# A fused attention, expert and scan network on one core: the blocks are divided twelve to four between the two sets of expert tiles instead of eleven to five

## What is computed

```
# 1 x = x + delta_rule_attention(norm(x))       16 heads of 16
# 2 expert layer: 32 experts, each token goes to 8 of them, plus a shared one
g = jnp.einsum('th,eih->eti', x, expert_gate)
u = jnp.einsum('th,eih->eti', x, expert_up)
outs = jnp.einsum('eti,ehi->eth', jax.nn.silu(g) * u, expert_down)
gathered = jnp.take_along_axis(outs_t, topk_idx[:, :, None], axis=1)
final = (gathered * topk_w[:, :, None]).sum(1)
# 3 state-space scan over the sequence: delta = softplus(x @ W_delta.T + b).mean(-1), h = dA * h + dB
# 4 quantized linear: the rows go to a 6-bit grid in blocks of 32, then x @ weight.T + bias
```

## Time and profile before

| | us |
|---|---|
| median of 3 runs | 3052.33 |
| lowest and highest | 3044.51, 3056.43 |
| the profiled execution | 3045.67 |
| its span, first to last instruction | 3043.5 |

### The profile page before, as it was taken

The page is one execution under the profiler, slowest core; times in us unless marked ns, Lnnn a source line. Parts: engine busy times, 40 slices in busy tenths (PEclk is TensorE's granted clock), DMA queues, the critical chain, the costliest instruction groups (busy, mean ns, idle before and its releaser), DMA issues. The chain is left out here.

```text
span 3043.5 us, 109358 instructions
## 1 busy us (share of the span) xinstructions
PE 2498.7 (82%) x45968; PEld 1887.2 (62%) x45968; DVE 2124.9 (70%) x5160; ACT 1605.3 (53%) x2896; POOL 1112.7 (37%) x1092
## 2 busy tenths in 40 slices
PE   4578887788888878788778999999978898987665
PEld 2345555556565555555566888888867676765443
DVE  4878988899889999888835222222325676878996
ACT  5454555555465554455124555555546666665442
POOL 0000233333333333233433777777744333332000
PEclk8778888888888898788679999999999899999877
DMA  2000122122222122113235999998798575754431
GB/s 66 8 11 10 49 74 71 53 79 75 71 74 73 55 79 73 63 69 111 84 114 172 301 310 305 306 305 296 258 336 305 202 275 209 268 217 173 161 107 28
DMA packets 191579, 448.61 MB, mean 147 GB/s; under 512 B 34034, under 2 KB 83700, under 8 KB 182772
## 3 DMA queue, kind: packets, MB, share of 16 engines
q1 hardware_dynamic: 129652, 284.26, 28.5%
q0 software_dynamic: 52224, 148.97, 12.9%
q10 hardware_dynamic: 9216, 8.39, 0.9%
HBM read 266.07 MB, written 175.42 MB: 145 GB/s over the span
## 5 line engine op out<-in xcount | busy, mean ns | idle before, releaser
L1041 POOL DMA_INDIRECT scr_xs<-xn_r,idx x512 | 534.1, 1043 | 1136.8 <-PE ps L473 479.7
L1068 POOL DMA_INDIRECT scr_ys<-y,idx_t x576 | 578.4, 1004 | 548.0 <-ACT sg L1333 253.1
L712 PE MATMUL ps<-xT,wr 128*128 128x256 f32 (+1 forms) x2560 | 563.5, 364 | 4.7 <-DVE h L2053 4.7
L2053 DVE TENSOR_TENSOR h<-sg,ps 128x256 f32<-128x256 f32 x320 | 125.2, 393 | 532.8 <-ACT sg L1333 532.2
L712 PEld LDWEIGHTS ps<-xT,wr 128*128 128x128 f32 x2560 | 439.1, 193 | 56.1 <-issue 14.1
L720 PE MATMUL ps<-wr,h 128*128 128x256 f32 x1152 | 312.3, 390 | 56.4 <-ACT y L1340 56.3
L1340 ACT ACTIVATE y<-ps,of_row 128x256 f32<-128x256 f32 x576 | 244.8, 471 | 145.2 <-PE ps L720 139.8
L720 PEld LDWEIGHTS ps<-wr,h 128*128 128x128 f32 x1152 | 218.5, 195 | 89.3 <-issue 62.1
L1680 DVE TENSOR_TENSOR tu<-tu,tmp 128x60 f32<-128x60 f32 (+14 forms) x480 | 242.5, 505 | 16.5
L527 PE MATMUL ps<-sq,w_proj 128*128 128x512 f32 x512 | 249.7, 624 | 5.1 <-issue 2.4
L1677 DVE TENSOR_TENSOR tmp<-tu 128x60 f32<-128x60 f32 (+14 forms) x480 | 241.6, 503 | 13.4
(11 more groups left out here) (268 smaller groups left out, 4231.6 us busy)
## 6 DMA issues: line engine op xcount, KB each, us to landing
wr<-in_wexp SPq DMA_DIRECT2D x224, 384.0 KB, 4.5
xt<-scr_xs SPq DMA_DIRECT2D x256, 280.0 KB, 4.2
yg<-scr_ys SPq DMA_DIRECT2D x64, 1024.0 KB, 7.4
scr_ys<-y,idx_t POOLq DMA_INDIRECT x576
scr_xs<-zeros SPq DMA_DIRECT2D x64, 140.0 KB
xt<-scr_xs SPq DMA_DIRECT2D x64, 140.0 KB
x_in<-in_x SPq DMA_DIRECT2D x64, 128.0 KB, 3.1
x_res<-in_x SPq DMA_DIRECT2D x64, 128.0 KB, 2.6
```

What stands on the lines that cost most here:

```text
L712: last = pe.matmul(ps[:, bank, half * TILE:half * TILE + wide], wr[:, w % NW, at:at + EI], xT2[:, t % NH, k, 0:wide], start=k == 0, stop=k ...
L1041: nc.gpsimd.indirect_dma_start(xs[int(i >= FIRST)][:, :], bass.IndirectOffsetOnAxis(idx[:, i % NR, c, k:k + 1], 0), xn_r[:, i % NR, c, :], ...
L1068: nc.gpsimd.indirect_dma_start(ys[int(t >= NTH[0])][:, :], bass.IndirectOffsetOnAxis(idx_t[:, t % NRT, r:r + 1], 0), y2[:, t % NY, r, :], ...
```

## The change

Two lines: the number of blocks whose rows go to the first table.

```
 def stages(j, NB):
 
     on = {s: j + ahead for s, ahead in (("A", 2), ("B", 1), ("C", 0), ("P", -1)) if 0 <= j + ahead < NB}
-    if "P" in on and on["P"] + 1 in (NB * 11 // 16, NB):
+    if "P" in on and on["P"] + 1 in (NB * 12 // 16, NB):
         on["H"] = int(on["P"] + 1 == NB)
     return on
...
     T = x.shape[1]
     NB = T // TB
     HALVES = 2
-    FIRST = NB * 11 // 16
+    FIRST = NB * 12 // 16
     NR = 3
     CAP = B * FIRST * TB + TILE
     ROUNDS = 8
```

## The result

| | before, us | after, us |
|---|---|---|
| median of 20 runs each, on one chip | 3051.17 | 3061.42 |
| lowest and highest | 3041.79, 3060.38 | 3046.96, 3072.43 |
| the profiled execution | 3045.67 | 3060.9 |
| its span | 3043.5 | 3058.8 |

The ratio is 1.0037, with an interval of 1.0026 to 1.0049: 11 us slower, clear of zero but inside the 0.5% that was counted as no change. The forecast was 10 us faster, so the direction was wrong as well as the size.

A forecast was written before the change was run, and what follows sets the result against it. PE bounds tiles alone, a DVE-PE-ACT loop the iterations with tiles, DVE those without. 48.5 - 2 - 40.7 + 17.8 - 33.9 = -10.3 us gave a median of 3042 us, range 3020 to 3068.

The forecast's parts named there:

- Sixteen tiles alone, and fewer ahead of the scan: Part two gains 16 full tiles, +48.5 us; the 34 slots ahead of the first scan hold fewer, -2 us.
- The iterations with tiles: Part three's loop: 10 iterations with 6 slots instead of 9 with 9, period 42 us, -40.7 us.
- the third and fourth leg: Loop through DVE, PE and ACT: softplus to `tile_step` 1.8 us, `tile_step` to the next scan 4.2 us.
- Scan to `off_tail`: First leg of the loop: DVE work with four tile steps, 20.6 us, PE's rows coming in time.
- `off_tail` to the end of the softplus: Second leg of the loop, over xa, turns and deltas with a slot in it: 15.5 us, between 14 and 16.6.
- The iteration where the tables change: DVE newly waits 15.4 us for chunk 48 behind the last tile's scatter; the iteration grows by 17.8 us.
- An iteration without tiles less: End of part three: four intervals without tiles instead of five, -33.9 us.
- A: Table-change iteration: the chunk is hidden, 41 us instead of 56.9; -26 us in all, 3026. Chance 0.12.
- B: Loop with tiles shrinks to 40 us or less if the second leg takes 14; -30 us, 3022. Chance 0.14.
- C: ACT's slot ahead of the softplus holds the loop near the straight line, 45.4 us; +24, 3076. Chance 0.14.
- D: PE's clock drops with less work, second leg 2 us a period longer; +10 in all, 3062. Chance 0.10.

The follow-up runs named there:

- six fillers: Changed kernel plus six matmuls that nothing reads, run by PE while it waits for `xa`: 1.0021 times the kernel before, usual interval with tiles 43.0 us.
- the gate ahead and four: Changed kernel with ACT's second slot ahead of the two norm roots and four unread matmuls in PE's wait for `xa`: 0.9978 times the kernel before.
- gate ahead of the roots: Changed kernel with ACT's second slot of an iteration run ahead of the two norm roots, not behind them: 1.0061 times the kernel before.
- Five slots ahead of iteration 0: Changed kernel with 39 slots instead of 34 ahead of iteration 0: 1.0047 times the kernel before, interval where tables change 39.8 us.

## Why the prediction was wrong

**Sixteen tiles alone, and fewer ahead of the scan: right.** +43.2 for +46.5. The six rounds that are alone grew by 6.1 us each, as forecast. The first and the last round, which run beside other work, grew by 5.2 and 3.4 us, and that is what is missing.

**The iterations with tiles: this step failed,** by 25.7 us, which is the whole miss (15.3 + 10.3 = 25.6). The mechanism held: the loop has the four legs, the 10.40 us stall is gone, and the third and fourth leg measure 1.8 and 4.4 us for 1.8 and 4.2. The first two were sized too short:

- *Scan to `off_tail`:* 21.65 for 20.6. I had added up DVE's work and looked only at PE's rows for what it might wait for. A gate stands on ACT behind two roots and a table load, and DVE waits 1.17 us for it.
- *`off_tail` to the end of the softplus:* 16.6 for 15.5. I took 15.5 from an iteration without a slot while writing that a slot stays in. And I read the leg of before in one iteration alone, where it is 16.6 us; in the other seven it is 14.3 to 15.0. What parts them is in PE's rows, which I hadn't read at this place. Here are the turns and the up pass in the iteration of the earlier trace rows, then in the one behind it, and the clock of the two places:

```profile
2564.20 1.92 PE L444 MATMUL ps<-identity,xa 128*128 128x128 f32 x8 [1.97 <-ACT xa L1114]
2565.91 2.78 PE L712 MATMUL ps<-xT,wr 128*128 128x256 f32 x8
2616.67 1.09 PE L444 MATMUL ps<-identity,xa 128*128 128x128 f32 x8 [0.59 <-ACT xa L1114]
2564.00:2567.30 3.30, 3.10 (x12) 2.84 (x13) 2.83 (x6) 2.59 (x7) 0.96 (x1) 0.54 1.01 395
2614.00:2619.00 5.00, 3.93 (x28) 3.46 (x28) 3.30 (x12) 5.00 (x13) 2.49 (x3) 1.00 0.89 361
```

Before, the turns took 1.92 us in this one iteration and 1.09 in the other seven. There the low clock stood elsewhere, at the end of an iteration, behind PE's wait for the emptied bank:

```profile
2630.84 1.19 PE L720 MATMUL ps<-wr,h 128*128 128x256 f32 x2 [4.93 <-ACT y L1340]
2630.50:2636.50 6.00, 5.66 (x38) 4.55 (x38) 5.76 (x10) 3.31 (x6) 3.58 (x4) 0.54 0.57 161
```

In the changed kernel PE's long wait is the one for `xa` (5.2 us an iteration for 1.3), and the turns take 1.97 us in eight of nine iterations. So the change took the low clock from the end of an iteration, where DVE has no wait behind it, to the start of the chain that ends in the scan. Kept at the full clock, the leg is 15.1 us with six fillers, and 14.5 with the gate ahead and four.

Eight of the nine periods are 44.4 to 44.7 us, 19.9 over the forecast together, and 2.15 us of each are these two legs. The one of 46.3 adds 4.3 (there PE's rows of the quantized layer came late, and DVE waited 2.2 us for them), and iteration 0, at 38.2 instead of 36.6, another 1.6. The gate ahead of the roots took the first leg's excess away and the fillers the second's; only both together gave 41.4. The gate alone gave 44.3, six fillers alone 43.

**The iteration where the tables change: right,** +17.9 for +17.8, and its wait 14.3 for 15.4. Five slots ahead of iteration 0 take it away.

**An iteration without tiles less: right,** -32.5 for -33.9.

**The rivals.** A is out: the chunk is not hidden. B's 40 was not reached, with 41.4 at the best. C's number, 45.4, was nearest to the period of 44.4, but its slot alone is not what holds it: moved away, it left 44.2. At the full clock its place counts a little, 41.6 us without it ahead of the softplus and 43.0 with it (six fillers). D gave the right time, 3062, and named the right engine, but the time is partly luck: it charged 2 us a period to the clock, where the leg came out 1.1 over the forecast, and another 1.05 came from the first leg, which D doesn't name. My argument against D, that the long stall goes, was wrong: PE's long wait went to another place. The Trainium skill's page TensorE: Matmul & The Clock Gate (Part 1: The HAM clock gate) says that the gate is throttled unless activity releases it; the trace agrees, with 1.00 ahead of the idle stretch, 0.50 and 0.51 in the stretches behind it (the changed kernel, and the gate ahead of the roots), and turns at 1.04 us when PE had been kept busy. The prediction had the slow stretches of D follow from less work overall. The granted clock of iterations 1 to 9 is 0.94, no lower than before (0.93): an average over the iteration hides a place that sets the end.

The Trainium skill's page ScalarE: Activation LUTs (What ACT_TABLE_LOAD costs) adds a drain of 1.38 us to a load. After, a load starts at 2619.45, takes 1.28, and its gate starts at 2620.74, 0.01 us behind its end: the trace shows no such drain, and going by the trace cost the forecast nothing.

The change as a whole moves 16 tiles at 2.7 us to where PE is the bound, and gets 6.5 us a period back (51.2 to 402.1 / 9 = 44.7) where DVE, PE and ACT wait for each other in turn. The places of three slots (one of PE's and two of ACT's) were worth more than the number of blocks in a table.

## What to carry to other kernels

When a loop runs through several engines, read every engine's rows at the joint where one leg ends and the next begins, and take a leg from an iteration that holds what the new one will hold. Taking out interleaved work gives back less than its share: see first where a long stall sits and which item's gate stands behind it, since moving that one item may be worth more. Read such a leg in several iterations and not in one. Where TensorE idles for some microseconds just ahead of matmuls that others wait for, as for 5.2 us here, reckon with the low clock for those matmuls, and see by a filler whether it pays to keep it busy.

## What was unexpected in the hardware

- Starting a chain earlier on PE gave nothing, to 0.1 us, in most iterations: the turns began 1.6 us earlier and the up pass behind them took 3.62 us instead of 2.55. The clock was low over 6.7 us instead of 3.3. In the one iteration in which it was low over 3.2, the period fell to 42.5 us.
- Matmuls whose results are thrown away, 3.60 us of them in each iteration, made the usual iteration 2.9 us shorter (44.3 to 41.4), and the mean of nine some 2.4 us (44.5 to 42.1).
- Between iterations of one kernel with the same order, a low clock at the place that others wait for made 2.6 us of 44.2.
- The first chip and the one on which before was repeated differ by 5.5% on that kernel, all of it ahead of the first scan (41 us in part one, 129 from the first gate to the first scan). DMA moved 240 GB/s beside the tiles instead of 306; whether that is the cause was not tested. The intervals in part three were the same within some 1.7 us.
